# First products of both MLPs in three float32r parts, with shared temporaries and a new written order

## The reference, cut to what matters

```python
def mlp(n, fc_w, proj_w):            # n 256x128, fc_w 128x512, proj_w 512x128
    h = jax.nn.relu(n @ fc_w)        # the first product
    return jnp.square(h) @ proj_w    # the second product
```

## Time and profile before

| | |
|---|---|
| device time, median of 3 runs | 925.98 us (922.77 to 926.07) |
| the profiled execution's own time | 926.01 us |
| its span, first to last instruction | 924.2 us |
| lies around the span | 1.8 us |
| mean granted TensorE clock | 0.993 of full speed |

### The profile page before, as it was taken

How to read it: one execution, slowest core, us unless ns; L and a number is a source line. 1 busy time by engine, 2 the same in 40 slices (tenths; PEclk the granted TensorE clock), 3 DMA queues, 4 the chain that set the end, 5 groups by cost and what they waited for, 6 DMA issues and landing times. The chain is left out here.

```text
span 924.2 us, 24882 instructions
## 1 busy us (share of the span) xinstructions
PE 876.6 (95%) x9248; PEld 754.2 (82%) x9248; DVE 670.8 (73%) x1867; ACT 550.5 (60%) x1192; POOL 383.7 (42%) x643
## 2 busy tenths in 40 slices
PE   2799999999999999999999999999999999999986
PEld 2587778888878888988989797988888888978775
DVE  7979889786877776787868677777688676668330
ACT  4545565846565856647386564637555765676841
POOL 1672343443244535334362543326252424553532
PEclk9999999999999999999999999999999999999998
DMA  8200000000000000000000000000000000000000
GB/s 281 87 2 18 8 7 2 7 2 2 19 2 8 13 2 18 8 12 14 2 19 2 18 2 1 19 1 13 2 2 2 12 1 15 1 13 1 13 12 12
DMA packets 17927, 15.71 MB, mean 17 GB/s; under 512 B 2065, under 2 KB 15761, under 8 KB 17553
## 3 DMA queue, kind: packets, MB, share of 16 engines
q1 hardware_dynamic: 17808, 14.12, 4.8%
HBM read 12.02 MB, written 2.10 MB: 15 GB/s over the span
## 5 line engine op out<-in xcount | busy, mean ns | idle before, releaser
L1167 PE MATMUL pool<-gH,w_h_hi 128*128 128x256 f32 x512 | 150.2, 293 | 4.4 <-POOL gL L535 2.2
L1167 PE MATMUL pool<-gH,w_h_lo 128*128 128x256 f32 x512 | 144.9, 283 | 0.0
L1167 PE MATMUL pool<-gL,w_h_hi 128*128 128x256 f32 x512 | 144.8, 283 | 0.0
L1061 DVE TENSOR_REDUCE mneg<-pool 128x2 f32<-128x512 f32 (+1 forms) x192 | 119.9, 683 | 26.3 <-PE pool L1167 25.9
L711 ACT ACTIVATE PT<-pool 128x512 f32<-128x512 f32 x192 | 102.3, 603 | 28.7 <-PE pool L1167 28.4
L629 ACT ACTIVATE BC<-pool 128x512 f32<-128x512 f32 x128 | 75.3, 603 | 68.0 <-PE pool L1167 65.3
L948 DVE TENSOR_TENSOR M<-pool,LM 128x512 f32<-128x512 f32 x128 | 87.6, 685 | 36.5 <-PE pool L1167 35.9
L1167 PE MATMUL pool<-BC 64*128 64x256 f32 (+1 forms) x1024 | 108.0, 345 | 1.9 <-DVE M L949 1.2
L494 POOL TENSOR_SCALAR_AFFINE_SELECT PT<-PT 128x256 f32<-128x256 f32 (+1 forms) x192 | 89.3, 486 | 39.9 <-ACT PT L711 37.8
L1167 PEld LDWEIGHTS pool<-BC 64*128 64x128 f32 x1024 | 87.4, 189 | 21.0 <-issue 11.1
L1167 PEld LDWEIGHTS pool<-gH,w_h_hi 128*128 128x128 f32 x512 | 97.2, 190 | 8.2 <-issue 3.8
(11 more groups left out here) (233 smaller groups left out, 2361.1 us busy)
## 6 DMA issues: line engine op xcount, KB each, us to landing
X<-in_x SPq DMA_DIRECT2D x16, 128.0 KB, 2.1
x<-in_x SPq DMA_DIRECT2D x16, 128.0 KB, 2.3
out<-ob SPq DMA_DIRECT2D x16, 128.0 KB, 2.0
hid<-in_w_h SPq DMA_DIRECT2D x1, 1024.0 KB, 8.6
gAB<-in_w_h SPq DMA_DIRECT2D x1, 1024.0 KB, 9.0
PT<-in_w_B SPq DMA_DIRECT2D x1, 512.0 KB, 5.0
PT<-in_w_C SPq DMA_DIRECT2D x1, 512.0 KB, 6.6
Qs<-in_s SPq DMA_DIRECT2D x1, 512.0 KB, 4.5
```

Of the source, the lines that this page charges most:

```text
L1061: v.reduce_max(dst, o, axis=AX.X, negate=True).then_inc(S["mx"], 1)
L1167: return p.matmul(o, lhsT, rhs, start=start, stop=True, skip_group_check=True)
```

## The change

1. `w_mfc` and `w_afc` get a float32r high part and remainder. Their DMAs go to raw buffers (`gate`, `val[:, 1]`), two more `phi` on ACT and two more `plo` on DVE (128x512 each) split them. `ga` of item 0 waits for the fourth `plo`, `conv` of item 1 for the fifth.
2. `t2c` and `t5c` write the float32r tiles `t2H` and `t5H`; new DVE parts `t2l` and `t5l` (one 128x256 subtraction each per item) write the remainders `t2L` and `t5L`. `up` and `upb` call `split_product`, and wait for the remainder. The PSUM banks of `t2` and `t5` are given back by the remainder, not by the copy.
3. `x2n` goes: `ln2` writes `l1`, and `ln1` of the next item waits for `t6` instead of `x1`. `ytm` goes: `yn` writes the first half of `yv`, and `yv` of the next item waits for `t4` instead of `yt`.
4. Raw data of the masks and of `r_a` land in `sqb` and `ro`, with one more wait on the folds each in `qk` and `rp` of item 0; `ident_bf` shrinks to 32 columns, made by four small copies.
5. All five written orders and the bank table are new. Apart from the 2 `phi`, 2 `plo`, 16 `t2l` and 16 `t5l`, they hold the same parts.

```diff
-    t2=(1, "t2c"), up=(1, "sq"), down=(1, "xa"), t3=(1, "t3c"), qkv=(1, "rp"), qt=(1, "qtc"), kt=(1, "ktc"), s=(4, "mx"),
+    t2=(1, "t2l"), up=(1, "sq"), down=(1, "xa"), t3=(1, "t3c"), qkv=(1, "rp"), qt=(1, "qtc"), kt=(1, "ktc"), s=(4, "mx"),
...
-    w_mfc, w_afc = sb("w_mfc", [P, HID]), sb("w_afc", [P, HID])
+    w_mfc, w_afc = split("w_mfc", HID), split("w_afc", HID)
...
-    t2s, t3s, t4s, t5s = (sb(f"t{n}s", [P, L]) for n in (2, 3, 4, 5))
+    t3s, t4s = sb("t3s", [P, L]), sb("t4s", [P, L])
+    t2H, t2L, t5H, t5L = (sb(f"t{n}{c}", [P, L], F32R) for n in (2, 5) for c in "HL")
...
+            elif k == 3:
+                act.wait_ge(in_c, 16 * 4)
+                a.activation(w_mfc[0][:], raw_mfc, ACT.Copy).then_inc(p_hi, 1)
+            elif k == 4:
+                act.wait_ge(in_d, 16 * 11)
+                a.activation(w_afc[0][:], raw_afc, ACT.Copy).then_inc(p_hi, 1)
...
         def ga(i, _):
             act.wait_ge(S["gat"], at("gat", i))
-            if i >= 1:
+            if i == 0:
+                act.wait_ge(p_lo, 4)
+            else:
...
-            a.activation(t2s[:], bank("t2", i)[:, 0:L], ACT.Copy).then_inc(S["t2c"], 1)
+            a.activation(t2H[:], bank("t2", i)[:, 0:L], ACT.Copy).then_inc(S["t2c"], 1)
...
-                act.wait_ge(S["yt"], at("yt", i - 1))
+                act.wait_ge(S["t4"], at("t4", i - 1))
...
+            elif k > 2:
+                w, raw = (w_mfc, raw_mfc) if k == 3 else (w_afc, raw_afc)
+                v.tensor_tensor(w[1][:], raw, w[0][:].bitcast(F32), ALU.subtract).then_inc(p_lo, 1)
...
+        def t2l(i, _):
+            dve.wait_ge(S["t2c"], at("t2c", i))
+            v.tensor_tensor(t2L[:], bank("t2", i)[:, 0:L], t2H[:].bitcast(F32), ALU.subtract).then_inc(S["t2l"], 1)
...
-                v.tensor_tensor(ytm[:].rearrange("p (m s c) -> p m s c", s=2, c=PA), y[:, :, :, 0:PA],
+                v.tensor_tensor(yv[:, 0:L].rearrange("p (m s c) -> p m s c", s=2, c=PA), y[:, :, :, 0:PA],
...
-                dve.wait_ge(S["x1"], at("x1", i - 1))
+                dve.wait_ge(S["t6"], at("t6", i - 1))
             normed(1, 5, i, l1, xa[:, i % 2]).then_inc(S["ln1"], 1)
...
-            normed(2, 6, i, x2n, x1[:, i % 2]).then_inc(S["ln2"], 1)
+            normed(2, 6, i, l1, x1[:, i % 2]).then_inc(S["ln2"], 1)
...
         def up(i, k):
-            pe.wait_ge(S["t2c"], at("t2c", i))
+            if i == 0 and k == 0:
+                pe.wait_ge(p_lo, 4)
+            pe.wait_ge(S["t2l"], at("t2l", i))
             o, = claim("up", i, k)
             for b in range(2):
-                last = mm(o[:, b * L:(b + 1) * L], w_mfc[:, (2 * k + b) * P:(2 * k + b + 1) * P], t2s[:], b == 0)
+                last = split_product(o[:, b * L:(b + 1) * L], w_mfc, (2 * k + b) * P, t2H[:], t2L[:], b == 0)
```

More of the change, by code:

```diff
@@ L32 @@
     yt=1, t4=1, o=1, t5=1, upb=2, downb=1, t6=1, w1=2, w2=2, h1=2, h2=2, w3=1,
-    ss1=1, xnhi=1, ga=1, val=1, xp=1, bcx=8, ss2=1, t2c=1, relu=2, ss3=1, t3c=1, qk=1, vv=1, qtc=2, ktc=1,
-    ex=12, yv=1, t4c=1, ss4=1, t5c=1, relub=2, t6hi=1, sl=2, ghi=2, ge1=2, hhi=2, ge2=2,
+    ss1=1, xnhi=1, ga=1, val=1, xp=1, bcx=8, ss2=1, t2c=1, t2l=1, relu=2, ss3=1, t3c=1, qk=1, vv=1, qtc=2, ktc=1,
+    ex=12, yv=1, t4c=1, ss4=1, t5c=1, t5l=1, relub=2, t6hi=1, sl=2, ghi=2, ge1=2, hhi=2, ge2=2,
     st0=1, ag0=1, xh=1, xm=1, nrm=1, xnlo=1, conv=4, m=8, yg=1, xm2=1, xa=1, e2=1, nw=14, rp=3, qs=2, mx=12, mh=2, qm=4, yn=2,
@@ L41 @@
     tin=(1, "xnlo"), inv=(1, "conv"), gat=(1, "ga"), vt=(1, "xp"), bc=(1, "bcx"), cb=(2, "m"), v=(1, "yg"), out=(1, "xm2"),
-    t2=(1, "t2c"), up=(1, "sq"), down=(1, "xa"), t3=(1, "t3c"), qkv=(1, "rp"), qt=(1, "qtc"), kt=(1, "ktc"), s=(4, "mx"),
-    mt=(1, "qm"), e=(4, "ex"), pv=(1, "yv"), yt=(1, "yn"), t4=(1, "t4c"), o=(1, "xa2"), t5=(1, "t5c"), upb=(1, "sqb"),
+    t2=(1, "t2l"), up=(1, "sq"), down=(1, "xa"), t3=(1, "t3c"), qkv=(1, "rp"), qt=(1, "qtc"), kt=(1, "ktc"), s=(4, "mx"),
+    mt=(1, "qm"), e=(4, "ex"), pv=(1, "yv"), yt=(1, "yn"), t4=(1, "t4c"), o=(1, "xa2"), t5=(1, "t5l"), upb=(1, "sqb"),
     downb=(1, "xa3"), t6=(1, "t6lo"), w1=(1, "sl"), w2=(1, "gt"), h1=(1, "ge1"), h2=(1, "ge2"), w3=(1, "ln3"))
@@ L100 @@
-        "ex ex bcx bcx bcx val yv vv t6hi xp bcx bcx sl sl ga qtc ktc qtc bcx bcx ghi ghi t4c bcx ss4 ge1 hhi ge1 t5c hhi ex "
[6 rows of a table removed]
+        "pxx ss1 pex pex pex pex pex xnhi phi pex phi phi phi phi pex pex ga bcx bcx ss1 bcx bcx bcx bcx val bcx bcx xp xnhi "
+        "fhi fhi bcx bcx fhi bcx fhi fhi val fhi bcx xp bcx t2c ss2 fhi bcx bcx ss1 relu bcx relu ga xnhi t3c ss3 qk vv bcx "
+        "bcx bcx t2c ss2 fhi ss1 relu relu bcx bcx val bcx xp ga t3c ss3 qk qtc ktc qtc bcx bcx fhi xnhi bcx bcx bcx ex ex ex "
@@ new lines @@
+        "ex ga val ss2 t2c xp ex ex ex ex relu relu ss1 bcx bcx ex ex ex ex bcx vv fhi bcx yv bcx t4c xnhi qtc ktc t5c ga ss2 "
+        "qtc ss4 t2c relub bcx relub bcx bcx bcx bcx val ss1 xp bcx bcx ss3 bcx t3c ex t6hi ex ex ex qk sl sl ex ex ex ex ghi "
+        "ghi xnhi relu relu ex ex ex ex ge1 vv yv ga ss2 val hhi bcx t4c bcx qtc ktc t2c t5c ge1 qtc xp hhi relub bcx relub "
+        "ss4 ge2 ge2 ss1 relu relu ex t3c ex ex ex bcx ss3 ex ex ex ex t6hi qk ex ex ex bcx ex sl sl ghi ghi bcx bcx vv yv "
@@ L107 @@
+        "bcx ge1 hhi ktc qtc ge1 xnhi hhi qtc t4c ge2 t5c ge2 relub relub ss4 bcx bcx val bcx ex ex ex ex bcx bcx xp t2c ss3 "
[9 rows of a table added]
+        "bcx t2c ghi t5c ss4 relu ga ge1 relu ge1 hhi hhi ktc qtc qtc relub ss1 bcx relub val bcx ge2 ge2 xp bcx ex ex ex ex "
[11 rows of a table added]
     ),
     DVE=(
-        "st0 dec ag0 m01 dec xh dec xm dec dec dec nrm plo plo plo st0 xnlo plm plm ag0 plm fold conv conv conv xh m plm conv "
[36 rows of a table removed]
+        "dec st0 ag0 dec m01 dec xh dec xm dec dec st0 nrm ag0 plm plm st0 plm xh xm xnlo plm plm plo plo plo ag0 plo plo "
@@ L146 @@
+        "conv conv plm conv plm m plm m conv nrm fold fold fold m m xnlo m m m m conv conv yg st0 conv ag0 conv m st0 xh xm2 "
[36 rows of a table added]
     ),
     Pool=(
-        "zero r1 r1 r2 r2 r1 r1 r1 r2 r2 r1 xr fsc fsc fsc fsc flo fsc fsc flo fsc gp fsc fsc flo fsc xr flo xr flo flo zero "
[3 rows of a table removed]
-        "r8 r8 sel r4 r4 sel sel sel sel sel sel sel outp glo glo hlo hlo r8 r8 r5 r5 gp sel sel sel r1 sel r6 r6 x1 sel xr "
-        "sel r4 sel sel r7 r7 xr r4 sel sel sel sel glo glo r1 r1 xr hlo hlo r5 r5 outp r2 r2 r3 r3 r6 r6 sel sel sel sel gp "
@@ L166 @@
[L166 to L172 removed]
+        "zero r1 r1 r2 r2 r1 r1 r1 r1 r2 r2 xr fsc fsc fsc fsc fsc fsc flo fsc gp flo flo flo xr flo flo xr fsc fsc fsc r2 r3 "
[3 rows of a table added]
@@ new lines @@
+        "r6 r8 r8 xr outp sel sel xr sel sel x1 r3 hlo hlo r7 r7 r4 r4 r8 r8 glo glo r3 outp r5 r5 r6 r6 sel sel sel x1 sel "
+        "hlo hlo r7 r7 sel sel sel sel r4 r4 sel sel sel sel r8 r8 glo glo hlo hlo outp sel sel sel r5 r5 sel sel r6 r6 x1 "
+        "sel sel r7 r7 sel sel sel sel sel glo glo r8 r8 r5 outp r5 hlo hlo r6 r6 x1 r7 r7 r8 r8 outp glo glo hlo hlo r8 r8 "
+        "outp"
+    ),
+    SP=(
+        "loadx loadx loadx loady loady loadx loadx store loady loadx loadx loady loadx store loady store store loadx loadx "
+        "loady loady store loadx store loady store loady loadx loadx store loady store loady loady store loady store loady "
+        "store loady store loady store store store"
@@ new lines @@
+    "7132467132416723153416732450167670134526343520174014570164562356234560123456201345601523460106534260753420103456"
+    "7035467013530124670156340123456701231245671243567412367451236745123601562347015623052367035621453671245361012345"
+    "0107645237640253760234567124567241567234567231675231523025016750123467023450172324360130645106323514062351040123"
+    "4560123456023407564230173650415074157012301452367230167234507126450176204517604512734512673456712124567124230214"
+    "1254014230167423401236146725301647253165473016547205632471234567234523674523201453043565701234501230456721045367"
@@ L190 @@
+    "3014567013450134675301674252153062741623574603450167401235647401723015236701451234567123145167234516723450710123"
+    "6457013045673206173427142367230160761450671523067105235670123567015230650172345601570235140671234567312456723456"
+    "0723730134512670452014675201467501465701645012463054123605412522012341412524167240156271450627145206714503267101"
+    "45326572301453061374562031745623012475601034752063475634032401045010101023401010"
 )
@@ L314, in program, with flat @@
     ep2, junk = sb("ep2", [P, T]), sb("junk", [P, 4, T, D], BF16)
+    def flat(ap):
+        return ap.rearrange("p a c -> p (a c)")
     raw_in, raw_B, raw_C = yv[:], PT[:, 0:2, :], PT[:, 2:4, :]
@@ L323, in program @@
     diff, causal = xr[:, 0].rearrange("p t d -> p (t d)"), xr[:, 1].rearrange("p t d -> p (t d)")
-    r_ms, r_mm, r_as, r_am, r_w3 = t4s[:, 0:D], t4s[:, D:], t5s[:, 0:D], t5s[:, D:], l1[:, 0, :]
-    raw_mask = (t2s, t3s)
```

(37 more changed lines are left out.)

58 lines of the change are left out of this document (20 added, 38 removed), and 182 rows, old and new, of tables (Activation, DVE, PE, Pool).

## The result

The changed kernel takes **911.91 us** (median of 4 runs, 910.56 to 912.42), against 925.18 us for the kernel before (4 runs, 922.77 to 926.07): ratio 0.9866, 95% interval 0.9844 to 0.9889. That is 13.3 us less; forecast were 10.5 less, to 915.5. The profiled execution took 912.08 us, its span is 910.3. The total is near the forecast, but as will be seen two things that the prediction did not have, of about 7 and 9 us, pull it in opposite directions. All times here are of runs near full clock; one of the ten runs of the last experiment (1085.09 us, mean clock 0.753) is left out.

The account below looks back on a forecast made before the run. PE, busy 95%, was taken as the bound, with ACT and DVE setting the start and one item's chain the end. 926.0 - 10.0 (products) - 1.0 (start) + 0.5 (end) = 915.5 us; range 909 to 922.

Parts of the forecast that it names:

- The products: `up` and `upb` on PE: three split matmuls at 0.118 us replace two float32 passes at 0.216, saving 10.0 us.
- The rival that they save nothing: Three weight loads cost what two float32 passes do, so 926 us, plus or minus 2; chance 0.03.
- The new waits in the middle: 110 to 850 us: remainders delay `up` and `upb` by 0.5 to 1.2 us, hidden by other items' work; cost nothing.
- that rival: PE waits for DVE's remainders at each of 32 places, 0.52 us each, 16.6 us in all: 932 us; chance 0.08.
- The start: Up to item 0's last `v`: `inv` 3.8 us later, but absorbed, so that `v` comes 1.0 us earlier.
- The walk: Following ACT's and DVE's queues through the start by durations: `m0` at 29, `m1` 31, `m2` 38, `m7` 43 us.
- PE's idle from its `inv` to 110 us: Sign of being wrong, at the start: this idle above 9.9 us less the 3.8 of the later start.
- The end: Bare chain of items 14 and 15: a `t5l` each, +0.5 us taken, bounds 0 and +1.5.
- the rival in which the order gains more: Order gains 2.6 us at the start, 2 in the middle, 1 at the end: 911 us; chance 0.15.

Follow-up runs that it names:

- the last experiment: The kernel before with 192 unused bytes per partition ahead of `mask_bf`, nothing else changed: 921.98 us, ratio 0.9965.

## Why the prediction was right in its number, and where it was wrong

**The products: right in the stream, half of it in the time.** The three matmuls do start 0.113 to 0.118 us apart with their own weights each, and in the same order PE's stream is 9.3 us shorter with them (forecast 10.0). The rival that they save nothing is refuted by the same rows. (Its estimate has a float32 pass at 213 ns; no row gives that figure, the step in the earlier trace rows is 216.) In medians the split is worth 5.3 us. Of the missing 4 us the two traces put 3.0 in the rest of the stream, beside a stretch at half clock from 96 to 103 us, and the single runs put only about 1 us on the clock; the rest is open.

**The new waits in the middle: right at nothing, for a reason the prediction gave no room.** PE waits 0.3 us for the remainders. But I held them covered by what PE has of other items, whatever the order; the order of before does not cover them, where the split loses 5.4 us. I gave that rival 0.08 as a matter of DVE's queue. What it lacked was the question which part of the change buys the cover. The new order is that part, and the doubled remainders show that it buys about as much as is needed: 0.42 us more at each, and PE waits 3.2 us more.

**The start: wrong.** `inv` starts at 20.84 us (forecast 21.3), and the first two `m` at 28.49 and 30.21 (29 and 31). The walk failed at the third: 38 forecast, 43.47 measured, and the eighth at 50.51 in place of 43. I walked the queues with each fold at its time alone. The rows gave the warning, an `xh` at 1.93 us for two small instructions and a fold at 1.77, since these stood beside POOL, and I didn't look at POOL's timeline. With the collision taken away the third `m` comes at 36.29 and the eighth at 41.79, 1.7 and 1.2 us ahead of the walk's own numbers. The term was -1.0; measured, the eighth `m` is 4.95 us later than before (50.51 against 45.56), and taking the stall away gives 8.6 us back. The prediction said that it would be wrong if PE's idle from its `inv` to 110 us were above 9.9 - 3.8 = 6.1 us. It is 11.8, of which one wait is 7.6.

**What was not in the sum at all: where the tiles lie.** 6.9 us in the kernel before, 4.5 in the changed one. I had priced the buffers at nothing because nobody waits for them.

**The end: right.** 0.7 us more of idle in the last 70.3 us, forecast +0.5.

**The sum.** By the medians the 13.3 us fall into three parts, one experiment after the other: 7.4 for the new buffers and places (old order, float32), 0.6 for the new order, 5.3 for the split products in it. The forecast of 10.5 was 0, 0.5 and 10.0. So the places, 7.4 us that the sum did not have, made up for 4.7 us that the products did not bring, and the order's 0.6 is what is left of its gains after the stall, whose removal gives 8.6. The total landed in the range by luck: two of its three parts are off by more than 4 us. Without the stall the kernel is at 903.3, below the range of 909 to 922; at the place of the kernel before it would be 4.5 to 6.9 us slower, 908 to 910 (an estimate from the two shifts). That is nearest to the rival in which the order gains more, 911.

**The better version.** The changed kernel with one `plm` moved is at 903.31 us, 2.35% below the kernel before and 8.6 us below the changed one. With all tiles 64 bytes on it is at 902.77, within the spread of the same.

## What to carry to other kernels

Before pricing a step that is moved on DVE, lay POOL's timeline beside it: an instruction with all its operands in SBUF cost about the length of POOL's instruction there (1.23 to 1.75 us), however small it was. When a change that adds work to a chain comes with a new written order, ask what each would be worth without the other. And when tiles change their size, look at the distance of unchanged matmuls in a full stream before and after: if it moved, a part of the result has nothing to do with the change's idea.
